# Second attention: values of two head pairs summed together in four of eight slots, and one slot for the next input's turn

## The reference, cut to what matters

```python
x = x + L0_xattn(layernorm(x), ctx)      # first attention
x = x + L0_ffn(layernorm(x))             # mixture of experts, top 2 of 8
x = x + L1_xattn(layernorm(x), ctx)      # second attention: the change is here
x = x + L1_ffn(layernorm(x))             # second expert layer

def L1_xattn(x, context):                # 16 heads of 64
    xn = layernorm(x) * gamma + beta
    q = xn @ w_q
    k, v = split(context @ w_kv)
    attn = softmax(q / 8 @ k.T)          # per head, 256 x 256
    return (attn @ v @ w_out + b_out) * tanh(gate)
```

## Time and profile before

| what | us |
|---|---|
| median of three runs | 1995.46 (1993.36 to 1995.59) |
| the profiled execution in all | 1989.19 |
| its span, first to last instruction | 1987.4 |
| first attention, 0 to 550 in the trace, about | 550 |
| expert layer, 550 to 1175, about | 625 |
| second attention, 1175 to 1756, about | 581 |
| second expert layer, the rest, about | 231 |

### The profile page before, as it was taken

How to read it: one execution, slowest core, us unless ns; L and a number is a source line. 1 busy time by engine, 2 the same in 40 slices (tenths; PEclk the granted TensorE clock), 3 DMA queues, 4 the chain that set the end, 5 groups by cost and what they waited for, 6 DMA issues and landing times.

```text
span 1987.4 us, 41321 instructions
## 1 busy us (share of the span) xinstructions
PE 1778.9 (90%) x15920; PEld 1483.4 (75%) x15920; DVE 1419.8 (71%) x2887; ACT 1129.6 (57%) x2812; POOL 775.8 (39%) x1160
## 2 busy tenths in 40 slices
PE   4788888889899899999999959999999999997646
PEld 3555656657899899999999847888878878876522
DVE  4667777774280489889888468999999999667421
ACT  1344555553334677777777456777777777743310
POOL 2202221101001233333332067788888887644000
PEclk8789999999999899999999979999999999998767
DMA  6434444322687576676676742222222221112599
GB/s 193 107 76 86 86 86 84 83 71 102 218 306 246 181 262 235 239 248 239 227 262 227 246 125 64 65 85 65 65 86 65 65 86 59 48 46 87 188 370 332
DMA packets 134116, 298.70 MB, mean 150 GB/s; under 512 B 13152, under 2 KB 77408, under 8 KB 118688
## 3 DMA queue, kind: packets, MB, share of 16 engines
q1 hardware_dynamic: 111520, 186.18, 30.2%
q0 software_dynamic: 18048, 105.69, 15.5%
q10 hardware_dynamic: 4352, 4.20, 0.6%
HBM read 207.93 MB, written 87.82 MB: 149 GB/s over the span
## 4 chain that ended last, share of the span: by engine, by line
PE 71%; DVE 13%; DMA 7%; issue 3%; POOL 3%; ACT 2%; SPq 1%; POOLq 0%; DVEq 0%
PE ps L1193 11%; PE ps L1207 11%; PE ps L1787 5%; PE ps L352 5%; PE ps L214 4%; PE ps L1818 4%; PE ps L1807 4%; PE ps L1773 4%; PE ps L358 3%; DMA R<-rp_scratch 2%; PE ps L454 2%; DVE NM L591 2%; DVE NM L180 2%; PE ps L443 2%; PE ps L431 2%
## 5 line engine op out<-in xcount | busy, mean ns | idle before, releaser
L191 ACT ACTIVATE P<-ps,NM 128x256 f32<-128x256 f32 x512 | 235.6, 473 | 156.8 <-DVE NM L180 156.6
L204 POOL TENSOR_TENSOR P<-P,RS 128x1024 f32<-128x1024 f32 x128 | 246.4, 1925 | 88.9 <-DVE RS L198 88.6
L591 DVE TENSOR_REDUCE NM<-ps 128x2 f32<-128x512 f32 x256 | 164.6, 686 | 110.9 <-PE ps L431 110.8
L1193 PE MATMUL ps<-XRP,W1P 128*128 128x256 f32 x1872 | 227.2, 281 | 2.7 <-DVE W1P L1277 2.7
L702 ACT ACTIVATE PT<-ps 128x512 f32<-128x512 f32 x256 | 138.7, 593 | 150.2 <-PE ps L443 147.9
L1193 PEld LDWEIGHTS ps<-XRP,W1P 128*128 128x128 f32 x1872 | 220.4, 190 | 3.3 <-DVE W1P L1277 3.3
L1207 PE MATMUL ps<-W2P,HP 128*128 128x256 f32 x1872 | 221.3, 277 | 0.0
L1207 PEld LDWEIGHTS ps<-W2P,HP 128*128 128x128 f32 x1872 | 217.7, 188 | 0.0
L138 POOL TENSOR_TENSOR LTMP<-RSTD 128x2 f32<-128x2 f32 (+1 forms) x156 | 32.3, 207 | 349.8 <-DVE RSTD L131 341.5
L180 DVE TENSOR_REDUCE NM<-ps 128x2 f32<-128x512 f32 x256 | 164.2, 683 | 1.2 <-PE ps L1773 0.5
L1241 ACT ACTIVATE HF<-ps,WE 128x256 f32<-128x256 f32 x312 | 128.9, 465 | 44.6 <-PE ps L1193 44.6
(11 more groups left out here) (220 smaller groups left out, 3840.6 us busy)
## 6 DMA issues: line engine op xcount, KB each, us to landing
k_scratch<-KVS SPq DMA_DIRECT2D x64, 256.0 KB, 3.1
KS<-k_scratch SPq DMA_DIRECT2D x64, 256.0 KB, 3.5
V<-v_scratch SPq DMA_DIRECT2D x16, 1024.0 KB, 6.5
rp_scratch<-RP SPq DMA_DIRECT2D x16, 1024.0 KB, 9.2
R<-rp_scratch SPq DMA_DIRECT2D x16, 1024.0 KB, 14.0
QS<-q_scratch SPq DMA_DIRECT2D x96, 128.0 KB, 4.3
v_scratch<-KVS SPq DMA_DIRECT2D x48, 256.0 KB, 2.3
ys_scratch<-YS SPq DMA_DIRECT2D x39, 256.0 KB, 8.2
```

The source lines that it names most:

```text
L191: i = e.activation(self.P[u % 4][:, c, :], PS[SB[n % 3]][:, y * 256:y * 256 + 256], ACT.Exp, bias=self.NM[:, u % 4, c:c + 1], accum_out=se ...
L204: e.tensor_tensor(p, p, self.RS[:, u % 4, :].unsqueeze(2).to_broadcast([128, 4, 256]), ALU.mult).then_inc(self.s_pn, 1)
L591: e.tensor_reduce(NM0[b % 2][:, :, 8 * h + p], PS[SB[(2 * u + h) % 3]][:, :].rearrange("p (l j) -> p l j", l=2), AX.X, ALU.max, negate=Tru ...
L1193: m = e.matmul(PS[p][:, hh * 256:hh * 256 + 256], W1P[i % 2][wi][:, cc * 1024 + hc * 128:cc * 1024 + hc * 128 + 128], XRP[i % 2][xi][:, cc ...
```

## The change

A table `VALUES_AT` says in which slots values are summed, and of which pairs: two pairs in r0, r2, r5 and r7, none in r1, r3, r4 and r6 (one pair alone in slots 5 and 131). The pairs take both halves of bank `OB`: columns 0 to 255 for the first, 256 to 511 for the second. VectorE splits both in the slot behind, after the second one is summed. Both halves of the next input are turned in slot r3, where no values are summed, into the two halves of the same bank, and both are scaled in r4 after both turns. The turn of a half no longer waits for the scaling of the half before. The number of matmuls, transposes and VectorE instructions is the same.

```diff
+    VALUES_AT, u = {}, 0
+    for i in range(5, SLOTS):
+        n = 1 if i in (5, U + 3) else 2 if i % 8 in (0, 2, 5, 7) else 0
+        if n and u < U:
+            VALUES_AT[i] = list(range(u, min(u + n, U)))
+            u += n
+    TURN_AT = 3
...
-        def values(u, turned):
+        def values(u, first, turned):
             b, p = u // 8, u % 8
+            c0 = 256 * (u - first)
             w.wait_ge(d_vl[b % 2], 16 * (b // 2 + 1))
             w.wait_ge(a1.s_tv, 2 * u + 2)
-            w.wait_ge(a1.s_ot, 2 * u)
+            w.wait_ge(a1.s_ot, 2 * first)
             w.wait_ge(s_xh, turned)
...
-                    m = e.matmul(PS[OB][64 * h:64 * h + 64, 0:256], V1[b % 2][:, jt, (2 * p + h) * 64:(2 * p + h) * 64 + 64],
+                    m = e.matmul(PS[OB][64 * h:64 * h + 64, c0:c0 + 256], V1[b % 2][:, jt, (2 * p + h) * 64:(2 * p + h) * 64 + 64],
...
         def turn_x(b, cc, split):
             w.wait_ge(s_xn1, 2 * b + 2)
-            w.wait_ge(s_xh, 2 * b + cc)
             w.wait_ge(a1.s_ot, 2 * split)
             for lt in range(2):
-                m = e.transpose(PS[OB][:, 256 + lt * 128:384 + lt * 128], XN1[:, lt, cc * 128:cc * 128 + 128], ident)
+                m = e.transpose(PS[OB][:, cc * 256 + lt * 128:cc * 256 + lt * 128 + 128], XN1[:, lt, cc * 128:cc * 128 + 128], ident)
...
-            now = turned
-            if r in (2, 3) and is_batch(g + 1):
-                turn_x(g + 1, r - 2, max(0, i - 4))
-                turned += 1
-            if 0 <= i - 4 < U:
-                values(i - 4, now)
+            if r == TURN_AT and is_batch(g + 1):
+                for cc in range(2):
+                    turn_x(g + 1, cc, summed)
+                turned += 2
+            for u in VALUES_AT.get(i, ()):
+                values(u, VALUES_AT[i][0], turned)
+                summed = u + 1
...
         def scale_x(b, cc):
...
-            w.wait_ge(s_xt1, 2 * b + cc + 1)
+            w.wait_ge(s_xt1, 2 * b + 2)
...
-        def values_split(u):
+        def values_split(u, pair):
             hi, lo = (z[:, u % 8, :] for z in OT1[u // 8 % 2])
-            w.wait_ge(a1.s_pv, u + 1)
+            out = PS[OB][:, 256 * (u - pair[0]):256 * (u - pair[0]) + 256]
+            w.wait_ge(a1.s_pv, pair[-1] + 1)
...
-            if 0 <= i - 5 < U:
-                values_split(i - 5)
-            if r in (3, 4) and is_batch(g + 1):
-                scale_x(g + 1, r - 3)
+            for u in VALUES_AT.get(i - 1, ()):
+                values_split(u, VALUES_AT[i - 1])
+            if r == TURN_AT + 1 and is_batch(g + 1):
+                for cc in range(2):
+                    scale_x(g + 1, cc)
```

More of the change, by code:

```diff
@@ L1831, in pe_l1 @@
         w.wait_ge(s_kve, 128)
-        turned = 2
+        turned, summed = 2, 0
         for i in range(SLOTS):
@@ L1890, in scale_x @@
             w.wait_ge(d_w0_w1, 96)
-            w.wait_ge(s_xt1, 2 * b + cc + 1)
+            w.wait_ge(s_xt1, 2 * b + 2)
             w.wait_ge(s_qm1, 4 * (b - 1))
             for out in (half(XN1, cc), halves(hi[:, cc, :])):
-                i = e.tensor_scalar(out, halves(PS[OB][:, 256:512]), GB[:, 0, cc:cc + 1], GB[:, 1, cc:cc + 1], ALU.mult, ALU.add)
+                i = e.tensor_scalar(out, halves(PS[OB][:, cc * 256:cc * 256 + 256]), GB[:, 0, cc:cc + 1], GB[:, 1, cc:cc + 1], ALU.mult, ALU.add)
             i.then_inc(s_xh, 1)
@@ L1900, in queries_low @@
             e.tensor_tensor(lo, QB[:, :], hi.bitcast(fp32), ALU.subtract).then_inc(s_qb, 1)
-        def values_split(u):
+        def values_split(u, pair):
             hi, lo = (z[:, u % 8, :] for z in OT1[u // 8 % 2])
-            w.wait_ge(a1.s_pv, u + 1)
+            out = PS[OB][:, 256 * (u - pair[0]):256 * (u - pair[0]) + 256]
+            w.wait_ge(a1.s_pv, pair[-1] + 1)
             w.wait_ge(s_om, 2 * (u // 8 - 1))
-            e.tensor_copy(hi, PS[OB][:, 0:256]).then_inc(a1.s_ot, 1)
+            e.tensor_copy(hi, out).then_inc(a1.s_ot, 1)
             w.wait_ge(a1.s_ot, 2 * u + 1)
-            e.tensor_tensor(lo, PS[OB][:, 0:256], hi.bitcast(fp32), ALU.subtract).then_inc(a1.s_ot, 1)
+            e.tensor_tensor(lo, out, hi.bitcast(fp32), ALU.subtract).then_inc(a1.s_ot, 1)
         def result_add(b, lt):
```

## The result

The changed kernel takes 2022.83 us (median of 4 runs, 2017.34 to 2025.79) against 1994.41 (4 runs, 1992.14 to 1995.59) for the kernel before, measured beside it: 28.4 us or 1.4% more by the medians, and a ratio of 1.0157 [1.0134, 1.0179]. The ratios of this document are those on record, over the fast runs, with a 95% interval, and differ from the quotient of two medians by 0.15% at most. The forecast was 1994.1, with a range from 1986.5 to 2000. The profiled execution took 2025.79 us.

What follows compares the result with a forecast made beforehand. TensorE was taken to set the pace, VectorE close behind. Inputs 2 to 12 -3.0, g = 13 -0.5, g = 14 +0.2, g = 15 +1.5, head +0.4: -1.4 us, giving 1994.1 us on the median, range 1986.5 to 2000.

Steps and rivals of the forecast that it cites:

- TensorE's prices: TensorE: pair of values 1.87 us, slots r0 and r2 5.27, r3 4.04, r5 5.23, r7 5.47; saving 0.60 an input.
- The rival that a second block costs its full 1.01: Values pairs on TensorE: the second block pays 1.01 us like a separate one; about 5 us more, 1999; chance 0.08.
- The queue of VectorE: VectorE's bunched splits and scalings: r1 3.71 us (stall 0.35), r4 3.71 (0.31), r6 chain 3.50 (0.10), r3 no stall.
- The head, g = 0 and 1: First two inputs: VectorE sets the pace and the second split stands ahead of its queue; +0.4 us.
- only TensorE's work counts: Second attention: VectorE and GpSimd keep up, fourteen inputs save 0.60 us each; -8.4 us, 1987; chance 0.25.
- GpSimd's stretch: GpSimd from the start of r3 to r6's low half, release included: 14.14 us, with no idle time left.
- The stall in front of the queries of r6: TensorE in r6, waiting for GpSimd's low half: the old stall of 0.67 us shrinks to 0.25.
- The rival for "slower": GpSimd's r3 to r6 becomes the loop's clock; with 0.2 us per normalisation 7.2 us above forecast, 2001; chance 0.15.
- The step that failed: VectorE's addition in r5: held to the end of GpSimd's normalisation; r6's splits start at 13.42 us, r7's scores at 16.81.
- the signs that I had named for being wrong: Loop slots: r1 or r4 don't stall, GpSimd has idle time between r3 and r6, or r3 stalls too.
- the stalls in my sum: TensorE: 0.35 us in r1, 0.31 in r4, 0.25 or 0.10 in r6; in the last input 1.63 in r6.
- The last input: g = 15: r6 has 1.87 us of TensorE work for a chain of 3.50, stall 1.63; +1.5 us in all.

Runs made afterwards that it cites:

- e9_spread: Changed kernel with r5's addition ahead of queries_low, and VectorE's second splits (r0, r1, r6) and r4's second scaling moved later: 1978.87 us, ratio 0.9947.

## Why the prediction was wrong, point by point

**TensorE's prices were right.** A pair of values takes 1.88 us (1433.02 to 1434.90; forecast 1.87). Slots r0 and r2 measure 5.28 (5.27), r3 4.04 to 4.08 (4.04), r5 5.22 to 5.29 (5.23), r7 without clock fall 5.48 (5.47). The rival that a second block costs its full 1.01 is out.

**The queue of VectorE was right where GpSimd isn't beside it.** r1 is 3.70 (3.71), with a wait for the low queries, r4 3.72 (3.71), with a wait for an exponential, r3 without a stall. r6 of g = 14 and 15 is 3.50 (3.50). g = 13 takes 36.28 us and g = 14 36.31 (forecast 36.37 and 36.38). The head, g = 0 and 1, cost 0.3 us more (0.4), but that is luck: it takes 76.2 to 81.1 us in the traces of this study, and in the changed kernel 1.5 us of it are a clock fall behind a stall of 1.71 us. The rival "only TensorE's work counts" is out as well.

**GpSimd's stretch was nearly right.** From the scores of r3 to the end of the low half plus release I summed 14.14; it is 1435.86 + 0.06 - 1421.87 = 14.05, since the low half took 0.75 instead of 0.91. The stall in front of the queries of r6 was 0.1 us, not 0.25. The rival for "slower" was this stretch being stretched by VectorE. It had the right place and the wrong victim: GpSimd was on time, and VectorE paid.

**The step that failed** is the one on VectorE's addition in r5: "it is held to its end", the normalisation's, which put r6's splits at 13.42 and r7's scores at 16.81 (r6 3.83 us; measured 5.78). The mechanism, one engine holding the other, was the right one and even the starting times were: the normalisation began at 1433.26 - 1421.87 = 11.39 (I had 11.32). The size was wrong. The splits started at 15.44 instead of 13.42, since the hold went on through the low half and the low keys. I took the hold of the earlier trace rows, to the end of one normalisation, as the price of an addition beside GpSimd. It was the price in a state where GpSimd had waited for its input. Two lines earlier I had written that in the new order "GpSimd has no idle time left in this stretch", and didn't ask what that does to the engine that shares something with it. The experiments with the gather moved, with the backlog put into the kernel before and with the wait show from three sides that the length of the hold goes with GpSimd's state. It costs 1.95 us in each of eleven inputs. None of the signs that I had named for being wrong showed it: r1 and r4 stall, r3 doesn't, and GpSimd has no gap above 0.15 us from r3's normalisation to the low keys of r5.

The Trainium skill (GPSIMD Engine Reference, Key points), which the prediction cites, says that the two engines contend when a VectorE instruction has two SBUF inputs. The Trainium skill (SBUF — State Buffer, section "SBUF: two separate sides") says more: of a VectorE instruction with two SBUF inputs and a GpSimd instruction that reads SBUF, the one that starts first has the shared pair of ports for its whole length, and the other is fully blocked. The single holds agree (1.75 us, to the end of the running instruction). By this rule the hold in r5 would have ended with the normalisation, at some 2.2 us (2.16 in the kernel with the wait); measured are 4.10. The measurement decides: the end of the running instruction is not always the end of the hold.

**What was in no rival** is the clock. Seven of eleven stalls of 2.2 us on TensorE are followed by a slot at a granted clock of 0.76 that takes 1.6 us longer, together 10.9 us. Apart from one in the last input, the stalls in my sum were tenths of a microsecond, so I had no case for it; it came on top of the first error.

**The sum.** Forecast: -1.4 us. With +21.5 for the hold and +10.9 for the clock that makes +31.0; from the first scores to the end of the span it is 854.7 against 825.8 us, +28.9. The head, the inputs 2 to 12 less those two terms, g = 13 and g = 14 agree with their terms within 0.2 us. The last input takes 30.1 us to its last scores against 29.7; a pair of values then moves behind them, so some 0.9 us more were due in what follows, and 0.9 less were measured. The stages there are untouched, and I put the 1.8 us down to their spread (235.0 to 242.8 us from the last scores to the end in the traces of this study); no run was made for it.

**What stays open.** Every long hold in the loop was one in which GpSimd's normalisation had stood ready for 0.36 to 0.48 us behind something else, with the next instruction ready behind it. But not every such row makes one. In `e9_spread` the row in r4 was ready for longer, 1.0 us, and the addition got in behind the normalisation in all eleven inputs. In the changed kernel's r4 it is held only to the normalisation's end too, as it is in the head of both kernels, where at 1229.52 of the kernel before it starts during a gather, with the low half ready behind the normalisation, and takes 2.46 us. The order of the starts doesn't decide either: at 1237.18 of the changed kernel's head an addition that starts beside a gather, 0.55 us ahead of the normalisation, takes 2.77 us, and one at the same distance takes 0.45 in the kernel with the addition ahead. Which state of the queue decides was not found. Nor was it found why the clock fell in seven inputs and not in the four between them, after the same 2.2 us of idle time.

## What to carry to other kernels

The price of an instruction beside another engine holds for the state in which it was measured: if a change removes the partner's idle time, ask which of your instructions share something with it, and bound their price by the whole row of queued instructions, not by one. Where VectorE has an instruction with two SBUF inputs in such a stretch, place it so that it is over before GpSimd's next instruction starts, beside a gather for example (0.45 us instead of 4.10 here), or break GpSimd's row with a wait (2.16). Read its length in the trace afterwards, for a start ahead of the row was not always enough. A bunching that TensorE gains from must be followed through every queue behind it, and a stall that grows to microseconds can cost the clock as well.

## What the runs showed of the hardware that I had not expected

- A VectorE instruction with two SBUF inputs can be held through three GpSimd instructions in a row: 4.10 us for 1.91 + 0.75 + 1.29, and 0.45 us in eleven inputs where it ran beside a gather. A long hold ended 0.28 to 0.30 us after the last of them each time.
- In the long holds it makes no difference whether VectorE starts 0.03 or 0.52 us behind the first of the row. GpSimd isn't slowed in such a row: the low half takes 0.75 us there, and 0.91 to 0.95 where VectorE gets in at its start.
- After 2.2 us without work on TensorE the granted clock had a mean of 0.76 over the next slot r7 (6.96 to 7.10 us) in seven of eleven inputs, and in other seven of eleven with eight copies; after 0.95 us (the low keys moved) and 1.28 us (the backlog in the kernel before) it stayed at 1.00. One of 1.71 us in the changed kernel's head was followed by such a fall, and one of the same length in the kernel with the addition ahead wasn't.
